# Two graph layers in fp32 on one core: the written-out order of the pieces drawn anew, with a list for each engine at both ends

## What is computed

```python
# layer 0: one head
h = x @ W                                   # 512 -> 256
e = leaky_relu(h @ a0 + (h @ a1).T, 0.2) + (-1e9) * (1 - adj)
x = layernorm(x + concat([softmax(e) @ h, h]))
# layer 1: eight heads of 64
q, k, v = x @ Wq.T + bq, x @ Wk.T + bk, x @ Wv.T + bv
s = where(adj == 0, -inf, q @ k.T / 8)
x = layernorm(x + (softmax(s) @ v) @ Wo.T + bo)
```

## Time and profile before

| | |
|---|---|
| median of 3 runs | 3135.08 us (3133.39 to 3146.21) |
| the profiled execution | 3133.3 us, its span 3131.5 us |
| mean granted TensorE clock | 0.988 |
| matmuls busy | 2970.1 us (95%) |
| weight loads busy | 2504.4 us (80%) |
| VectorE, ScalarE, GpSimd busy | 2670.4, 2445.5, 2040.9 us |
| DMA | 685.39 MB, 219 GB/s |

### The profile page before, as it was taken

One profiled execution on the slowest core, in us unless ns is written; L12 is line 12 of the kernel. 1 busy time (PEld: TensorE's weight loads), 2 busy tenths in 40 slices (PEclk: granted clock), 3 DMA queues, 4 the chain that ended last, 5 costly groups with the idle time before them and its releaser, 6 DMA issues.

```text
span 3131.5 us, 58284 instructions
## 1 busy us (share of the span) xinstructions
PE 2970.1 (95%) x19084; PEld 2504.4 (80%) x19084; DVE 2670.4 (85%) x6556; ACT 2445.5 (78%) x5031; POOL 2040.9 (65%) x1415
## 2 busy tenths in 40 slices
...
GB/s 124 199 217 219 231 242 220 216 219 216 241 231 219 219 218 226 231 234 216 220 222 220 233 233 221 216 219 230 231 229 216 218 220 231 242 219 218 213 207 159
DMA packets 306413, 685.39 MB, mean 219 GB/s; under 512 B 56896, under 2 KB 90432, under 8 KB 273344
## 3 DMA queue, kind: packets, MB, share of 16 engines
...
## 4 chain that ended last, share of the span: by engine, by line
PE 71%; DVE 14%; issue 7%; ACT 5%; DMA 1%; POOL 1%; DVEq 0%; SPq 0%; ACTq 0%; POOLq 0%
PE R_bank L729 41%; PE O_bank L818 11%; PE S_bank L799 9%; PE L_bank L729 6%; PE L_bank L720 4%; DVE blocked L1115 3%; DVE stats L995 3%; DVE prob L1095 2%; DVE tokens L1083 2%; ACT qk_pair L859 1%; DVE o_half L1123 1%; DVE alpha L1040 1%; DVE x1T L991 1%; DVE qk_pair L1012 1%; ACT alpha L891 1%
## 5 line engine op out<-in xcount | busy, mean ns | idle before, releaser
L1175 POOL TENSOR_TENSOR turned_lo_prob<-turned_lo_prob,turned_hi_prob 128x1024 fp32r<-128x1024 f32 x512 | 1250.2, 2459 | 539.1 <-ACT turned_hi_prob L846 539.0
L934 ACT ACTIVATE prob<-prob,small_cols 128x512 f32<-128x512 f32 x1024 | 730.8, 715 | 228.8 <-DVE small_cols L1095 222.3
L1115 DVE STREAM_TRANSPOSE blocked<-prob 128x512 f32<-128x512 f32 x1024 | 696.4, 697 | 113.9 <-PE O_bank L818 59.4
L1095 DVE CUSTOM_DVE_ANT_0 prob<-S_bank,mask 128x512 f32<-128x512 f32 x1024 | 678.3, 681 | 35.5 <-PE S_bank L799 31.2
L846 ACT ACTIVATE turned_hi_prob<-turned_lo_prob 128x1024 fp32r<-128x1024 f32 x512 | 528.1, 1050 | 46.0 <-PE O_bank L818 29.8
L818 PE MATMUL O_bank<-turned_hi_prob,v_st 128*128 128x256 f32 x2048 | 521.7, 292 | 38.4 <-POOL turned_lo_prob L1175 38.3
L818 PE MATMUL O_bank<-turned_lo_prob,v_st 128*128 128x256 f32 x2048 | 507.6, 285 | 0.0
L799 PE MATMUL S_bank<-qk_pair 64*128 64x512 f32 x3072 | 444.8, 414 | 22.6 <-DVE small_cols L1095 19.7
L818 PEld LDWEIGHTS O_bank<-turned_hi_prob,v_st 128*128 128x128 f32 x2048 | 394.3, 193 | 79.2 <-POOL turned_lo_prob L1175 63.2
L729 PE MATMUL R_bank<-wv,x1T 128*128 128x256 f32 x3072 | 401.3, 286 | 0.2
L818 PEld LDWEIGHTS O_bank<-turned_lo_prob,v_st 128*128 128x128 f32 x2048 | 395.5, 193 | 4.2
...
## 6 DMA issues: line engine op xcount, KB each, us to landing
scratch<-blocked SPq DMA_DIRECT2D x256, 1024.0 KB, 4.1
turned_lo_prob<-scratch SPq DMA_DIRECT2D x256, 1024.0 KB, 5.6
tokens<-xT SPq DMA_DIRECT2D x128, 256.0 KB, 5.1
tokens<-x SPq DMA_DIRECT2D x128, 256.0 KB, 3.1
r_wide<-r_scratch SPq DMA_DIRECT2D x512, 64.0 KB, 3.4
out<-tokens SPq DMA_DIRECT2D x128, 256.0 KB, 4.1
r_scratch<-r_cols SPq DMA_DIRECT2D x256, 16.0 KB
tokens<-adj SPq DMA_DIRECT2D x1, 1024.0 KB, 6.8
```

What stands on the lines that cost most here:

```text
L934: act.activation(prob_tile(R, s), prob_tile(R, s), ACT.Exp, bias=negmax[:, slot:slot + 1], scale=-1.0, accum_out=psum_row[:, ph % 2, j:j + ...
L1095: dve.tensor_tensor_reduce(prob_tile(R, s), score_bank(R, s)[:, :], mask[:, s % 8 // 2, :], -SCALE, HUGE, ALU.add, ALU.min, negmax[:, slot ...
L1115: dve.transpose(blocked[:, ph % 2, :, :, 2 * (s % 2) + s % 4 // 2, :].rearrange("p d c i -> p c d i"), prob_tile(R, s).rearrange("p (d c i ...
L1175: pool.tensor_tensor(lo_ap, lo_ap.bitcast(F32), turned_hi_prob[:, 2 * a:2 * a + 2, :, :].bitcast(F32), ALU.subtract).then_inc(p_lo, 1)
```

## The change

No instruction's kind, size or operands change, and no wait is taken out of a piece. The ten tables of a round and of the last round are new, and START, PROLOGUE and ENDING become a list for each engine. In tables only two lines are shown; the rest is of the same kind.

```diff
 TENSOR_PLAN = (
-    "k1 N weigh",
-    "weigh scores scores",
-    "A3 C0 O0",
...
+    "N k1 weigh weigh C0 scores scores O0",
+    "O1 C1 O2 scores scores weigh weigh O3",
+    "q2 k2 D0 weigh weigh scores scores D1",
+    "W0 C2 W1 W2 W3 C3 D2 weigh",
...
-START = "A0 A1 A2 A3 B0 B1 B2 B3 w0 w1"
-PROLOGUE = """red0 N red1 red2 pre0 A0 pre1 pre2 red3 aexp0 aexp1 pre3 C0 aexp2 w2 C1 w3 aexp3 C2 evD0 evD1 D0 D1 lst0
...
+TENSOR_PROLOGUE = (
+    "N C0 C1 D0 C2 D1 C3 D2",
+    "D3 bb E0 E1 V0 E2 V1 E3",
+    "B0 q4 k4 V2 scores scores B1 scores",
+    "V3 B2 q1 B3 scores",
+)
+VECTOR_PROLOGUE = (
+    "red0 red1 red2 C0 red3 C1 evD0 w2",
+    "C2 lst0 evD1 C3 w3 bb evD2 lst1",
...
-            run_round(prologue, [PROLOGUE])
+            run_round(prologue, VECTOR_PROLOGUE)
             all_rounds(dve, run_round, LAST_VECTOR_PLAN)
-            run_round(end, [ENDING])
+            run_round(end, VECTOR_ENDING)
```

More of the change, by code:

```diff
@@ L77 @@
-    "B3",
[4 rows of a table added]
+    "weigh scores scores D3 q3 k3 weigh weigh",
[3 rows of a table added]
+    "scores weigh weigh B3 q1",
 )
 SCALAR_PLAN = (
[L80 to L111, removed]
[3 rows of a table added]
+    "exp C1 exp fin0 turn lows exp aexp2",
[6 rows of a table added]
+    "exp B0 exp exp exp A1 evQ4 turn",
+    "lows A2 B1 hi hi evV2 exp exp",
+    "exp evV3 A3 B2 turn exp exp lows",
+    "hi B3 exp hi turn",
@@ L112 @@
 )
 VECTOR_PLAN = (
[L114 to L131, removed]
```

270 lines of the change are left out of this document (86 added, 184 removed), and 54 rows, old and new, of tables (GPSIMD_PLAN, LAST_GPSIMD_PLAN, LAST_SP_PLAN, LAST_VECTOR_PLAN).

## The result

| | before | changed |
|---|---|---|
| median of the runs | 3134.23 us (3132.12 to 3146.21, 4 runs) | 3113.98 us (3111.21 to 3114.55, 4 runs) |
| ratio | | 0.993, 95% interval 0.9918 to 0.9942 |
| profiled execution, span | 3131.5 us | 3111.8 us |

A forecast was written before the change was run, and what follows sets the result against it. TensorE, with matmuls running 92.01 of 94.50 us a round, was taken as the bound. From 3133.3 us, -39 for the rounds and -3 for each end gave 3088 us, range 3052 to 3130.

The forecast's parts named there:

- the sum of the steady round: Wait-by-wait terms of a steady round: -1.3 us, between -2.4 and +0.2; times 30 rounds, -39 us.
- The wait at scores5: TensorE's wait for reduce7, which now precedes red0, goes: 0.44 idle plus 0.2 lost overlap, -0.6 us a round.
- The wait for qk_pair at D0: TensorE's wait for evQ2, 0.93 + 0.2, shrinks to 0.1 as VectorE comes earlier: -1.0 us a round.
- W3's wait: New wait for evW1 behind red3, up to 1.2 us if red is long; a third taken, +0.4 a round.
- The ends: First graph's new order -3 us (0 to -6); last graph's -3 us (+3 to -6).
- a gain in the first 134 us: Sign against the forecast: the gain sitting in the first 134 us or behind 3025 would make it wrong.
- The floor by the gap list: TensorE's idle gaps plus lost overlap leave 3.2 us a round, 96 in all; no order below about 3037 us.
- the 78 us of weight loads: Rejected measure of TensorE's fullness: 77.68 of 94.50 us, leaving 16.8 a round open, floor near 2630 us.
- The seam at weigh-2: TensorE's wait of 0.41 us for GpSimd's lo15; chain kept by the new tables, nothing won or lost.
- E1 to E3: E1's wait covered by scores13, -0.8; E2 and E3 wait 0.2 to 0.5 each, +0.7: -0.1 us a round.
- The wait only moves: Rival: evQ2 keeps its place, TensorE waits 1.13 + 1.55 at D0, round 94.3 to 94.8, 3130 us; chance 0.14.
- SP's queue: Slower rival: mv3 behind xt0 on SP lands late, delaying hi6 and weigh6; 3154 us; chance 0.1.

The follow-up runs named there:

- best version: y1 plus aexp2, C2, pre3 and red3 moved earlier and load xt1 directly behind mv4; 3065.28 us, 0.9774 of the kernel before.
- x4: Changed kernel with VectorE's red1 behind three reduce instead of directly behind sum-1; 3090.92 us, 0.9859 of the kernel before.
- x2: Changed kernel with VectorE's small step lrs behind sum2 instead of ahead of it; 3097.04 us, 0.9872 of the kernel before.
- y1: Changed kernel with both lrs behind sum2 and red1 behind three reduce on VectorE; 3076.24 us, 0.9807 of the kernel before.

## Where the prediction failed, and what it had right

The prediction was wrong in the size of the gain. The step that failed is the sum of the steady round: it had no term for the last products of O0 and none for weigh6, so both stood at nothing without a reason, and they came to 0.69 and 0.53 us of idle time in every round. The round was forecast to lose 1.3 us and lost 0.45 by D3's distance, which over 30 rounds is 26 us, all that the forecast is off by.

**Right, by its own terms.** The wait at scores5 went (0.44 of idle time). The wait for qk_pair at D0 went whole, 0.93, where 0.1 was left in the forecast. W3's wait came at 0.48, where a third of 1.2 was forecast; its cause, red3 beside lo4 and lo5, is the one named, though it is there in every round and not in a third. The ends: the first graph's lists gave about what was said (3 forecast, 2.4 and 4.8 in two traces), the last graph's nothing instead of 3. That 7.1 us ahead of the first D3 and 0.4 lost behind the last add up to what the ends were given is partly luck, and by the forecast's own signs a gain in the first 134 us spoke against it; 6.1 us sit there. The floor by the gap list held: the best version's round, 92.41, is still above the 91.4 of no wait at all, and no version came near the 78 us of weight loads.

**Better than forecast.** The seam at weigh-2 was put at "nothing won, nothing lost" and won 0.41: B2 stood ahead of sum6 on VectorE and does so no longer, which I had not read from the tables. E1 to E3 wait for nothing now, and scores12 for 0.26: a gain of 0.35 where the forecast had 0.1; the small waits that it named as a sign at E2 and E3 did not come.

**The step that failed.** The walk went from one wait that TensorE had before to the next, and asked of each whether it goes. Elsewhere it looked only at E, W3 and B. It did not ask which other cover (the work that TensorE still has in hand while its next input is made) was within half a microsecond of failing, and it took every duration other than `red`'s from its old place. Two covers did fail:

- O0, 0.69 us a round, which no term of the sum had. Before, red1 stood behind C0; directly behind sum-1 it lengthens GpSimd's norm-1 from 0.74 to 1.58. x4 shows it: 23 us.
- weigh6, 0.53 us a round, which no term had. lrs takes 2.0 for 0.2 and stands ahead of sum2. x2 shows it: 17 us.

With these two gone (y1) the kernel stands at 3076, below the forecast of 3088, since weigh-2's gain comes on top. Summed in idle time alone, the four old waits give -2.39 and the new ones +1.96, which is -0.43 of the -0.45. With the forecast's 0.2 for each wait the two missing terms are +1.62 and weigh-2's is -0.61; W3's is +0.68 where +0.4 stood.

**The range that I did not read.** The earlier trace rows gave `red` as anything from 1066 to 2789 ns, and I took a third between the ends. There was little to average: red1, red2 and red3 each had nearly the same length in every round, some 1.08 with GpSimd idle and, beside a `lo`, the rest of that `lo` plus 0.9 to 1.0. Before, red2 ran 2.33 us on average with GpSimd's first `lo` beside it for 1.38 of them; in the changed kernel red3 ran 2.18, with 1.22 of overlap. The position in the timeline gives the length, and both tables could have been laid side by side for that.

**The range.** Its two ends don't follow from the terms. With no new wait and the seam alone left, the round loses 3.2 - 0.6 = 2.6 us, not 2.4; with D0 unchanged, E's -0.1 and W3's 1.2 in full it grows by 0.5, not 0.2.

**The rivals.** "The wait only moves" (0.14) was nearest in its time, 3130, and in what happened, but it had the wrong place: not D0. That its time is near is luck: by its own numbers, D0's wait 1.55 longer and scores5's 0.6 gone, the round would be 0.9 us longer than before, not 94.3 to 94.8. SP's queue was real in kind (xt1 and mv5 rather than xt0 and mv3), and moving xt1 won 7 us, where that rival had it eat more than the whole gain; hi6, its sign, did not wait for its load in any of 27 rounds. The bound of "94.4 or more would make it wrong" was not reached with 94.14, and neither was 93.3.
